# Every fourth column per block: how a graph's turned tile goes through memory and back

## The chip, the core and the metric

The kernel runs on one core of one Trainium2 chip. The metric is the device time of one execution in microseconds (us). The core's engines run their own instruction streams and meet at semaphores: TensorE (PE in the profile), VectorE (DVE), ScalarE (ACT), GpSimd (POOL) and SyncE (SP), which here issues all the DMAs.

## What is computed

Two layers of masked attention with a layer norm ahead of each, on 128 graphs of 128 nodes with 384 features, in float32. Attention has 6 heads of 64.

```python
h = jnp.maximum(_layernorm(x, axis=-1), 0.0)
x = x + _L0_gnn_ref(h, Wq, bq, Wk, bk, Wv, bv, Wf, bf, adj)
h = jnp.maximum(_layernorm(x, axis=-1), 0.0)
x = x + _L1_gnn_ref(h, ...)          # the same with the second set of weights
# in each layer:
scores = jnp.einsum('bhqd,bhkd->bhqk', q, k) / np.sqrt(HEAD_SIZE)
probs = jax.nn.softmax(scores + bias, axis=-1)   # bias: 0 where adj, else -9e15
ctx = jnp.einsum('bhqk,bhkd->bhqd', probs, v)
return ctx @ Wf + bf
```

## The kernel before

A unit `t` is one group of four graphs (`PER`) in one layer; there are 64 units, 256 pairs of a graph and a layer. The two layers of different groups are interleaved. `over_slots` runs `slot(t)` for units 1 to 61 on every engine; each slot has four steps `i`, and each step does work of several graphs at different stages, chosen by `graph_at(t, i, steps)`. The order within a step is written out by hand in the `slot` function of each engine, and for the head and for the last two units (`last_units`) line by line.

Products of float32 data are made as three float16 products of high and low halves. For this each tile is split: ScalarE writes the high half, VectorE or GpSimd the low one.

Two tiles of each graph have to be transposed, with rows on the other axis: `h` (128 nodes x 384 features, the input of the projections) and the probabilities (128 queries x 6 heads x 128 keys, the right side of the context product). VectorE transposes only within blocks of 32 x 32, so the transposition has two parts:

- `turn_blocks` (lines 1229 to 1231; called by `h_turn` and `probs_turn`) turns 32 x 32 blocks on VectorE, from `h` into `h_blocks` or from the probabilities into `p_blocks`. Of each run of 128 columns, block `b` is made of the 32 neighbouring columns 32 b to 32 b + 31.
- the blocks are then moved across partitions by way of memory: `keep_blocks` (lines 356 to 361) writes the tile to `h_dram` or `p_dram` in one DMA, and `bring_back` (363 to 368) reads it into `h_moved` or `p_moved` with four DMAs, one for each group of 32 partitions. `keep_h`, `bring_h`, `keep_probs` and `bring_probs` call them from SyncE's stream.

The read tile is taken by ScalarE (`h_hi`, line 940, and `p_hi`, line 961), then by GpSimd (`h_lo`, 547, and `p_lo`, 552). In the first two units and the last three, where the probabilities aren't split, TensorE reads `p_moved` itself (`apply_probs`, 736). All buffers of this path (`h_blocks`, `h_moved`, `p_blocks`, `p_moved`) are double, by the parity of `i`. Each DMA adds 16 to its semaphore, so `h_back[i]` and `p_back[i]` grow by 64 for each tile.

On VectorE, `slot` runs the turn of the probabilities (line 1230) beside the residual add (1300), the low half of v (1258), the turn of h, the statistics (1225, 1227), the reciprocal of the softmax sums (1254), the masked scores with their minimum (1289), and the low halves of q and k (1269). The last are awaited by TensorE: the projections of q and k have two PSUM banks (`ps_qk`), and the scores of a unit need all six chunks. TensorE's projections and output products are lines 665 to 667, its context product line 759 and its scores line 779.

Of the kernel before, what the change touches and what calls it, by code (L numbers as in the profile page):

```python
# [21 lines left out]
def build(nc, x, adj, layers, out):  # L22
# [23 lines left out]
    SQ = 32  # L46
    QUADS = P // SQ
# [13 lines left out]
    def unit_no(t):  # L61
        return min(t, LAST)
# [17 lines left out]
    def unit_count(t, each=1, plus=0):  # L80
        return each * unit_no(t) + plus
# [10 lines left out]
    def wait(eng, sem, value):  # L92
        if value > 0:
            eng.wait_ge(sem, value)

    def graph_at(t, i, steps):

        return t + (i + steps) // PER, (i + steps) % PER
# [9 lines left out]
    def halved(t):  # L108

        return HALVED <= t < A - 1  # L110

    def halved_count(t, i):
        return PER * (t - HALVED) + i + 1
# [6 lines left out]
    with ExitStack() as ctx:  # L120
# [6 lines left out]
        def sem(name):  # L127
            return ctx.enter_context(nc.semaphore(name))
# [108 lines left out]
        h_back = [sem(f"h_back{i}") for i in range(PER)]  # L237
# [15 lines left out]
        p_back = [sem(f"p_back{i}") for i in range(PER)]  # L253
# [22 lines left out]
        def ctx_bank(i):  # L276
            return ps_shared[i % 2]
# [8 lines left out]
        def v_of(t, i):  # L286
            return v[:, (PER * t + i) % V_SLOTS, :]

        def v_part(t, i, part):
            return v_of(t, i).bitcast(F16)[:, part * H:(part + 1) * H]  # L290

        def p_part(i, part):
            return p_half[i % 2][:, part, :]
# [5 lines left out]
        def first_bank(i):  # L299

            return (ps_qk[0], ps_qk[1], ps_scores[0], ps_scores[1])[i]
# [6 lines left out]
        def moved_in_order(tile):  # L308

            return tile[:, :, :].rearrange("p a (c k) -> p c a k", c=KT)  # L310

        def in_order(view):
            return view.rearrange("p c (a k) -> p c a k", a=QUADS)
# [7 lines left out]
        def _(sp):  # L321
# [33 lines left out]

            def keep_blocks(t, i, blocked, blocks, dram, kept, back):

                wait(sp, back[i], unit_count(t, 16 * QUADS))
                wait(sp, blocked, unit_count(t, PER, i + 1))
                sp.dma_start(dram[i, :, :, :, :].rearrange("a r b n -> (a r) b n"), blocks[i % 2][:, :, :]  # L360
                             ).then_inc(kept[i], 16)

            def bring_back(t, i, dram, moved, kept, back):

                wait(sp, kept[i], unit_count(t, 16, 16))
                for quad in range(QUADS):
                    sp.dma_start(moved[i % 2][quad * SQ:(quad + 1) * SQ, :, :],  # L367
                                 dram[i, :, :, quad, :].rearrange("a r n -> r a n")).then_inc(back[i], 16)

            def keep_probs(t, i):  # L370
                keep_blocks(t, i, p_blocked, p_blocks, p_dram, p_kept, p_back)

            def bring_probs(t, i):
                du, di = graph_at(t, i, -2)
                if halved(du):

                    sp.wait_ge(p_set, halved_count(du, di))
                else:
                    wait(sp, ctx_summed, unit_count(t, PER, i - 1))
                bring_back(t, i, p_dram, p_moved, p_kept, p_back)  # L380

            def keep_h(t, i):

                keep_blocks(t - 1, i, h_blocked, h_blocks, h_dram, h_kept, h_back)
# [241 lines left out]
        def _(pe):  # L626
# [109 lines left out]
            def apply_probs(t, i):  # L736
                vu, vi = graph_at(t, i, 8)
                if i % 2 and vu < B:

                    pe.wait_ge(v_set, unit_count(vu, PER, vi + 1))  # L740
                else:

                    wait(pe, out_added, unit_count(t, PER, i - 1))
                    pe.wait_ge(v_set, unit_count(t, PER, i + 1))
                if (t, i) == (0, 0):
                    pe.wait_ge(largest_taken, LAYERS)
                    pe.wait_ge(out_bias_set, LAYERS)
                if halved(t):
                    pe.wait_ge(p_set, halved_count(t, i))
                    terms = [(v_part(t, i, a), p_part(i, b)) for a, b in ((0, 0), (1, 0), (0, 1))]  # L750
                else:
                    pe.wait_ge(p_back[i], unit_count(t, 16 * QUADS, 16 * QUADS))
                    terms = [(v_of(t, i), p_moved[i % 2][:, :, :].rearrange("p a n -> p (a n)"))]
                for c in range(PAIRS):
                    for k, (values, turned) in enumerate(terms):
                        turned = turned.rearrange("p (a s k) -> p s a k", a=QUADS, s=HEADS)
                        for odd in range(2):
                            hd = 2 * c + odd
                            mm = pe.matmul(ctx_bank(i)[odd * DH:(odd + 1) * DH, c * P:(c + 1) * P],  # L759
                                           values[:, hd * DH:(hd + 1) * DH], turned[:, odd * PAIRS + c, :, :],  # L760
                                           start=k == 0, stop=k == len(terms) - 1)
                mm.then_inc(ctx_summed, 1)
# [148 lines left out]
        def _(act):  # L911
# [17 lines left out]
            def h_hi(t, i):  # L929
                b, rows = unit_no(t) % 2, slice(i * NODES, (i + 1) * NODES)  # L930
                if i == 0:

                    wait(act, qk_projected, unit_count(t - 2, CHUNKS, CHUNKS))
                if t == 0:
                    act.wait_ge(first_turned, i + 1)
                    nc.scalar.activation(ht_hi[0][:, :, rows], first_bank(i)[:, 0:H].rearrange("p (c k) -> p c k", c=KT),
                                         ACT.Copy).then_inc(ht_hi_set, 1)
                    return
                act.wait_ge(h_back[i], unit_count(t - 1, 16 * QUADS, 16 * QUADS))
                nc.scalar.activation(in_order(ht_hi[b][:, :, rows]), moved_in_order(h_moved[i % 2]), ACT.Copy  # L940
                                     ).then_inc(ht_hi_set, 1)

# [12 lines left out]
            def p_hi(t, i):  # L955
                if (t, i) == (HALVED, 0):

                    act.wait_ge(weights_set, CAST_ORDER.index(1) + 1)
                act.wait_ge(p_back[i], unit_count(t, 16 * QUADS, 16 * QUADS))
                act.wait_ge(ctx_summed, unit_count(t, PER, i - 1))  # L960
                nc.scalar.activation(p_part(i, 0), p_moved[i % 2][:, :, :].rearrange("p a n -> p (a n)"), ACT.Copy  # L961
                                     ).then_inc(p_hi_set, 1)
# [158 lines left out]
        def _(dve):  # L1121
# [105 lines left out]
                nc.vector.bn_aggr(mean_var[i % 2][:, :], stats[i % 2][:, :]).then_inc(mean_found, 1)  # L1227

            def turn_blocks(out, view, cols):
                return nc.vector.transpose(out.rearrange("p b (c k) -> p b c k", c=cols),  # L1230
                                           view.rearrange("p (c b r) -> p b c r", c=cols, b=QUADS))

            def h_turn(t, i):
                du, di = graph_at(t, i, -2)
# [269 lines left out]
```

## Time and profile before

| | before |
|---|---|
| median of three runs | 1856.35 us (1855.97 to 1858.41) |
| the profiled execution | 1854.17 us |
| its span, first to last instruction | 1852.4 us |
| mean granted TensorE clock | 0.995 of full speed |
| TensorE, VectorE busy in the span | 98%, 88% |
| ScalarE, GpSimd busy in the span | 84%, 80% |
| DMA engines, mean busy share of the queue SyncE feeds | 65.3% |

The busy time of an engine is that of its instructions in one profiled execution. Matmuls are pipelined, so a busy TensorE has work in flight but isn't at its peak for that. Line numbers are those of the kernel before. "SPq" is SyncE's queue of DMA issues: its times are those of issuing, not of the transfer. The profiled execution stands 2.18 us below the median.

### The profile page before, as it was taken

The numbers are of one execution on the slowest core, as the hardware profiler recorded it, in microseconds if no ns is written. First come the engines' busy times: TensorE is split into PE (matmuls) and PEld (weight loads), VectorE is DVE, ScalarE is ACT, GpSimd is POOL, SyncE is SP. The second block draws the span as 40 slices with busy tenths as digits, with TensorE's granted clock in tenths as the row PEclk, the third lists the DMA queues.
The fourth block names the chain that finished last, engine by engine and source line by source line (L and its number), as shares of the span: only waits on it lengthen the run. The fifth ranks groups of instructions, "written<-read, shape, count | busy, mean of one in ns | idle before, by whom it ended". The sixth has DMA issues, their size and how long they took to land.

```text
span 1852.4 us, 54319 instructions
## 1 busy us (share of the span) xinstructions
PE 1822.2 (98%) x17210; PEld 1050.3 (57%) x17210; DVE 1630.8 (88%) x5555; ACT 1556.1 (84%) x4789; POOL 1485.9 (80%) x1777
## 2 busy tenths in 40 slices
PE   7899999999999999999999999999999999999998
PEld 3455555555555555555555555555555555555555
DVE  7988888899898898988989889888898988889876
ACT  5768888888888888888888888888888888888884
POOL 4668888888888888888888888888888888888772
PEclk8999999999999999999999999999999999999999
DMA  6646766667666666666666666666666666666655
GB/s 193 171 144 198 211 193 196 195 200 212 198 206 189 197 209 203 205 196 194 202 208 204 198 196 201 194 209 205 191 198 197 209 204 200 201 185 189 186 178 182
DMA packets 439943, 363.32 MB, mean 196 GB/s; under 512 B 207701, under 2 KB 406889, under 8 KB 439657
## 3 DMA queue, kind: packets, MB, share of 16 engines
q1 hardware_dynamic: 439656, 359.86, 65.3%
q8 instruction: 137, 2.24, 0.5%
q14 instruction: 150, 1.22, 0.2%
HBM read 184.30 MB, written 175.37 MB: 194 GB/s over the span
## 4 chain that ended last, share of the span: by engine, by line
PE 86%; DVE 4%; DMA 4%; SPq 3%; issue 2%; POOL 1%; ACT 1%; DVEq 0%; POOLq 0%; ACTq 0%
PE ps_qk L665 12%; PE ps_shared L665 12%; PE ps_shared L667 12%; PE ps_shared L666 12%; PE ps_qk L667 12%; PE ps_qk L666 12%; PE ps_shared L759 7%; PE ps_scores L779 7%; SPq L367 3%; DMA p_dram<-p_blocks 2%; DVE probs L1289 1%; DVE p_blocks L1230 1%; DVE qk_lo L1269 1%; POOL probs L540 1%; DMA p_half<-in_L_gnn_Wk 0%
## 5 line engine op out<-in xcount | busy, mean ns | idle before, releaser
L986 ACT ACTIVATE probs<-probs,row_min 128x128 f32<-128x128 f32 x1512 | 583.0, 390 | 2.5 <-DVE row_rcp L1254 1.5
L540 POOL TENSOR_TENSOR probs<-probs,row_rcp 128x768 f32<-128x768 f32 x252 | 371.4, 1474 | 214.1 <-DVE row_rcp L1254 213.9
L1289 DVE CUSTOM_DVE_ANT_0 probs<-ps_scores,mask,minus_scale 128x128 f32<-128x128 f32 x1512 | 429.5, 347 | 0.9 <-issue 0.6
L552 POOL TENSOR_TENSOR p_half<-p_moved,p_half 128x768 f16<-128x768 f32 x236 | 388.0, 1644 | 3.2 <-ACT p_half L961 3.2
L1269 DVE SCALAR_TENSOR_TENSOR qk_lo<-ps_qk,qk_bias,qk_hi 128x512 f16<-128x512 f32 x384 | 277.7, 747 | 60.1 <-ACT qk_hi L969 59.2
L986 ACT ACTIVATION_READ_ACCUMULATOR probs<-probs,row_min 128x1 f32 x1512 | 288.0, 191 | 0.0
L969 ACT ACTIVATE qk_hi<-ps_qk,qk_bias 128x512 f16<-128x512 f32 x384 | 258.3, 673 | 15.1 <-PE ps_qk L667 15.1
L1300 DVE SCALAR_TENSOR_TENSOR x_tile<-ps_shared,out_scale,x_tile 128x384 f32<-128x384 f32 x256 | 157.6, 616 | 123.5 <-PE ps_shared L667 122.1
L536 POOL TENSOR_TENSOR x_tile<-x_tile,out_bias 128x384 f32<-128x384 f32 x256 | 257.8, 1008 | 1.1 <-DVE out_bias L1213 1.1
L665 PE MATMUL ps_shared<-wf_hi,ct_hi 128*128 128x384 f16 x768 | 250.7, 326 | 2.4 <-DVE ct_lo L1263 2.4
L666 PE MATMUL ps_shared<-wf_lo,ct_hi 128*128 128x384 f16 x768 | 250.7, 326 | 0.0
L667 PE MATMUL ps_shared<-wf_hi,ct_lo 128*128 128x384 f16 x768 | 250.6, 326 | 0.0
L665 PE MATMUL ps_shared<-wv_hi,ht_hi 128*128 128x384 f16 x756 | 247.6, 327 | 0.0
L666 PE MATMUL ps_shared<-wv_lo,ht_hi 128*128 128x384 f16 x756 | 247.4, 327 | 0.0
L667 PE MATMUL ps_shared<-wv_hi,ht_lo 128*128 128x384 f16 x756 | 247.4, 327 | 0.0
L1230 DVE STREAM_TRANSPOSE p_blocks<-probs 128x768 f32<-128x768 f32 x252 | 244.0, 968 | 3.7 <-POOL probs L540 3.7
L547 POOL TENSOR_TENSOR ht_lo<-h_moved,ht_hi 128x384 f16<-128x384 f32 x252 | 234.1, 929 | 8.0 <-ACT ht_hi L940 8.0
L948 ACT ACTIVATE v<-ps_shared 128x384 f16<-128x384 f32 x236 | 115.7, 490 | 143.5 <-PE ps_shared L667 142.7
L665 PE MATMUL ps_qk<-ht_hi,wq_hi 128*128 128x512 f16 x576 | 219.7, 381 | 2.1 <-DVE qk_lo L1269 1.8
L665 PE MATMUL ps_qk<-ht_hi,wk_hi 128*128 128x512 f16 x576 | 219.3, 381 | 0.0
L666 PE MATMUL ps_qk<-ht_lo,wq_hi 128*128 128x512 f16 x576 | 218.8, 380 | 0.0
L667 PE MATMUL ps_qk<-ht_hi,wq_lo 128*128 128x512 f16 x576 | 218.8, 380 | 0.0
(144 smaller groups left out, 3973.2 us busy)
## 6 DMA issues: line engine op xcount, KB each, us to landing
p_dram<-p_blocks SPq DMA_DIRECT2D x256, 384.0 KB, 2.4
p_moved<-p_dram SPq DMA_DIRECT2D x1024, 96.0 KB, 2.3
h_dram<-h_blocks SPq DMA_DIRECT2D x252, 192.0 KB, 2.6
h_moved<-h_dram SPq DMA_DIRECT2D x1008, 48.0 KB, 2.0
x_tile<-in_x SPq DMA_DIRECT2D x128, 192.0 KB, 2.9
out_x<-x_tile SPq DMA_DIRECT2D x128, 192.0 KB, 2.7
adj_u<-in_adj SPq DMA_DIRECT2D x64, 64.0 KB, 2.5
wv_raw<-in_L_gnn_Wv SPq DMA_DIRECT2D x2, 576.0 KB, 5.0
```

The source lines that it names most:

```text
L536: nc.gpsimd.tensor_tensor(xs, xs, out_bias[l][:, :], ALU.add).then_inc(res_ready, 1)
L540: nc.gpsimd.tensor_tensor(probs_of(t, i), probs_of(t, i), row_rcp[i % 2][:, :].rearrange("p (a o) -> p a o", o=1) .to_broadcast([P, HEADS, ...
L547: nc.gpsimd.tensor_tensor(in_order(ht_lo[b][:, :, rows]), moved_in_order(h_moved[i % 2]), in_order(ht_hi[b][:, :, rows]), ALU.subtract).th ...
L552: nc.gpsimd.tensor_tensor(p_part(i, 1), p_moved[i % 2][:, :, :].rearrange("p a n -> p (a n)"), p_part(i, 0), ALU.subtract).then_inc(p_set, 1)
L665: pe.matmul(acc, a_hi, b_hi, start=first, stop=False)
L666: pe.matmul(acc, a_hi, b_lo, start=False, stop=False)
L667: return pe.matmul(acc, a_lo, b_hi, start=False, stop=last)
L969: nc.scalar.activation(qk_hi[b][:, chunk, :], ps_qk[chunk % QK_BANKS][:, :], ACT.Identity, bias=qk_bias[layer_of(t)][:, chunk // KT, chunk ...
L986: ins = nc.scalar.activation(tile[:, s, :], tile[:, s, :], ACT.Exp, bias=row_min[i % 2][:, s:s + 1], scale=-1.0, accum_out=row_sum[i % 2][ ...
L1230: return nc.vector.transpose(out.rearrange("p b (c k) -> p b c k", c=cols), view.rearrange("p (c b r) -> p b c r", c=cols, b=QUADS))
L1269: nc.vector.scalar_tensor_tensor(out=qk_lo[b][:, chunk, :], in0=ps_qk[chunk % QK_BANKS][:, :], scalar=qk_bias[layer_of(t)][:, chunk // KT, ...
L1289: ins = nc.vector.tensor_tensor_reduce(tile[:, s, :], score_bank(i, s // PAIRS)[:, (s % PAIRS) * P:(s % PAIRS + 1) * P], mask[b][:, i, :], ...
```

## The change

Block `b` of a run of 128 columns is now made of every fourth column, 4 r + b for r from 0 to 31. VectorE's turn has the same shape and the same output; its input is read with a step of four floats. In memory the row (r, b) of a turned tile then belongs to partition 4 r + b, so the whole tile is one pattern with 128 partitions outermost, and `bring_back` reads it with one DMA. `h_back` and `p_back` grow by 16 for each tile instead of 64, and the waits on them are counted anew. The content of `h_moved` and `p_moved` is the same as before.

```diff
--- before.py
+++ after.py
@@ -355,7 +355,7 @@
 
             def keep_blocks(t, i, blocked, blocks, dram, kept, back):
 
-                wait(sp, back[i], unit_count(t, 16 * QUADS))
+                wait(sp, back[i], unit_count(t, 16))
                 wait(sp, blocked, unit_count(t, PER, i + 1))
                 sp.dma_start(dram[i, :, :, :, :].rearrange("a r b n -> (a r) b n"), blocks[i % 2][:, :, :]
                              ).then_inc(kept[i], 16)
@@ -363,9 +363,8 @@
             def bring_back(t, i, dram, moved, kept, back):
 
                 wait(sp, kept[i], unit_count(t, 16, 16))
-                for quad in range(QUADS):
-                    sp.dma_start(moved[i % 2][quad * SQ:(quad + 1) * SQ, :, :],
-                                 dram[i, :, :, quad, :].rearrange("a r n -> r a n")).then_inc(back[i], 16)
+                sp.dma_start(moved[i % 2][:, :, :], dram[i, :, :, :, :].rearrange("a r b n -> (r b) a n")
+                             ).then_inc(back[i], 16)
 
             def keep_probs(t, i):
                 keep_blocks(t, i, p_blocked, p_blocks, p_dram, p_kept, p_back)
@@ -749,7 +748,7 @@
                     pe.wait_ge(p_set, halved_count(t, i))
                     terms = [(v_part(t, i, a), p_part(i, b)) for a, b in ((0, 0), (1, 0), (0, 1))]
                 else:
-                    pe.wait_ge(p_back[i], unit_count(t, 16 * QUADS, 16 * QUADS))
+                    pe.wait_ge(p_back[i], unit_count(t, 16, 16))
                     terms = [(v_of(t, i), p_moved[i % 2][:, :, :].rearrange("p a n -> p (a n)"))]
                 for c in range(PAIRS):
                     for k, (values, turned) in enumerate(terms):
@@ -936,7 +935,7 @@
                     nc.scalar.activation(ht_hi[0][:, :, rows], first_bank(i)[:, 0:H].rearrange("p (c k) -> p c k", c=KT),
                                          ACT.Copy).then_inc(ht_hi_set, 1)
                     return
-                act.wait_ge(h_back[i], unit_count(t - 1, 16 * QUADS, 16 * QUADS))
+                act.wait_ge(h_back[i], unit_count(t - 1, 16, 16))
                 nc.scalar.activation(in_order(ht_hi[b][:, :, rows]), moved_in_order(h_moved[i % 2]), ACT.Copy
                                      ).then_inc(ht_hi_set, 1)
 
@@ -956,7 +955,7 @@
                 if (t, i) == (HALVED, 0):
 
                     act.wait_ge(weights_set, CAST_ORDER.index(1) + 1)
-                act.wait_ge(p_back[i], unit_count(t, 16 * QUADS, 16 * QUADS))
+                act.wait_ge(p_back[i], unit_count(t, 16, 16))
                 act.wait_ge(ctx_summed, unit_count(t, PER, i - 1))
                 nc.scalar.activation(p_part(i, 0), p_moved[i % 2][:, :, :].rearrange("p a n -> p (a n)"), ACT.Copy
                                      ).then_inc(p_hi_set, 1)
@@ -1227,8 +1226,9 @@
                 nc.vector.bn_aggr(mean_var[i % 2][:, :], stats[i % 2][:, :]).then_inc(mean_found, 1)
 
             def turn_blocks(out, view, cols):
+
                 return nc.vector.transpose(out.rearrange("p b (c k) -> p b c k", c=cols),
-                                           view.rearrange("p (c b r) -> p b c r", c=cols, b=QUADS))
+                                           view.rearrange("p (c r b) -> p b c r", c=cols, b=QUADS))
 
             def h_turn(t, i):
                 du, di = graph_at(t, i, -2)
```

## Rows read from the trace of the kernel before

**Rows 1.** The page, part 1: busy us (share of the span) xinstructions.

```profile
PE 1822.2 (98%) x17210; PEld 1050.3 (57%) x17210; DVE 1630.8 (88%) x5555; ACT 1556.1 (84%) x4789; POOL 1485.9 (80%) x1777
```

**Rows 2.** Windows: stretch, its length, busy us of each engine (xinstructions), clock, DMA share, GB/s.

```profile
0.00:129.50 129.50, 110.96 (x756) 59.13 (x757) 111.56 (x338) 84.28 (x231) 73.04 (x117) 0.93 0.59 174
129.50:185.60 56.10, 53.66 (x522) 31.25 (x521) 47.44 (x163) 46.60 (x145) 45.70 (x55) 1.00 0.63 183
185.60:1756.10 1570.50, 1569.28 (x15115) 908.62 (x15113) 1401.71 (x4811) 1363.35 (x4195) 1322.03 (x1565) 1.00 0.67 199
...
1812.20:1852.40 40.20, 32.20 (x312) 19.75 (x306) 24.37 (x80) 17.02 (x64) 7.14 (x5) 1.00 0.61 197
```

**Rows 3.** Chain that ended last, in order of time: start us, us, what; TensorE's context products.

```profile
178.65 1.13 PE ps_shared L759 x36
...
515.15 1.13 PE ps_shared L759 x36
```

**Rows 4.** VectorE's waits from 185.6 to 1756.1: waited for, us, times, longest.

```profile
DVE x_tile L1300 <- PE ps_shared L667: 112.7, 200, 1.2
DVE qk_lo L1269 <- ACT qk_hi L969: 45.2, 72, 1.6
```

**Rows 5.** TensorE's waits in the same stretch, all of them.

```profile
PE ps_scores L779 <- DVE qk_lo L1269: 1.2, 2, 1.0
```

**Rows 6.** Timeline of SyncE's queue, one graph: start us, us, what, count of issues.

```profile
916.16 0.38 SPq L360 DMA_DIRECT2D p_dram<-p_blocks  x1
...
918.64 1.75 SPq L367 DMA_DIRECT2D p_moved<-p_dram  x4
920.49 1.81 SPq L367 DMA_DIRECT2D h_moved<-h_dram  x4
```

**Rows 7.** The page, part 6: DMA issues, count, KB each, median us from issue to landing.

```profile
p_dram<-p_blocks SPq DMA_DIRECT2D x256, 384.0 KB, 2.4
p_moved<-p_dram SPq DMA_DIRECT2D x1024, 96.0 KB, 2.3
...
h_moved<-h_dram SPq DMA_DIRECT2D x1008, 48.0 KB, 2.0
...
wv_raw<-in_L_gnn_Wv SPq DMA_DIRECT2D x2, 576.0 KB, 5.0
```

**Rows 8.** ScalarE's waits for the reads, from 185.6 to 1756.1.

```profile
ACT p_half L961 <- DMA p_moved<-p_dram: 10.2, 24, 1.1
ACT ht_hi L940 <- DMA h_moved<-h_dram: 9.0, 20, 0.9
```

**Rows 9.** Chain that ended last, the tail: start us, us, what.

```profile
1836.32 2.67 DMA p_dram<-p_blocks
...
1843.07 2.21 DMA p_moved<-p_dram
...
1845.41 0.88 PE ps_shared L759 x12
```

**Rows 10.** Timeline of the tail: start us, us, what, [idle before, releaser].

```profile
1836.47 0.98 DVE L1230 STREAM_TRANSPOSE p_blocks<-x_tile 128x768 f32<-128x768 f32 x1 [0.80 <-POOL x_tile L540]
...
1842.81 0.33 PE L667 MATMUL ps_shared<-wf_hi,ct_lo 128*128 128x384 f16 x1
```

**Rows 11.** ScalarE's waits from 129 to 186.

```profile
ACT p_half L961 <- DMA p_moved<-p_dram: 6.0, 4, 3.8
```

**Rows 12.** Groups by form: line, engine, operation, xcount | busy us, mean ns | idle before.

```profile
L1230 DVE STREAM_TRANSPOSE p_blocks<-probs 128x768 f32<-128x768 f32 x252 | 244.0, 968 | 3.7 <-POOL probs L540 3.7
...
L1230 DVE STREAM_TRANSPOSE h_blocks<-h 128x384 f32<-128x384 f32 x252 | 139.2, 552 | 2.2 <-ACT h L926 2.2
...
L1207 DVE SCALAR_TENSOR_TENSOR wv_lo<-wv_raw,w_scale,wv_hi 128x1152 f16<-128x1152 f32 x2 | 3.9, 1933 | 0.0
...
L1207 DVE SCALAR_TENSOR_TENSOR wk_lo<-wk_raw,w_scale,wk_hi 128x1152 f16<-128x1152 f32 x1 | 2.4, 2437 | 0.0
...
L1207 DVE SCALAR_TENSOR_TENSOR wk_lo<-p_half,w_scale,wk_hi 128x1152 f16<-128x1152 f32 x1 | 1.4, 1386 | 0.0
```

## The prediction, made before the changed kernel was run

> **What bounds the kernel now.** The page comes first: TensorE (PE) is busy for 1822.2 of 1852.4 us, VectorE (DVE) for 1630.8 [rows 1]. A share of the span mixes stages, so the windows come next. From 185.6 to 1756.1 us TensorE has work in flight for 1569.28 of 1570.5 us at full granted clock, VectorE for 1401.71, ScalarE for 1363.35, GpSimd for 1322.03 [rows 2]. TensorE's context product of a pair of graphs recurs every (515.15 - 178.65) / 24 = 14.02 us [rows 3], so one graph of one layer takes 7.011 us and the stretch holds 224 of them. VectorE works 1401.71 / 224 = 6.258 us of each and idles 0.753. The waits say what that idle time is: 112.7 us on TensorE's output product, 45.2 us on ScalarE's high half of q and k [rows 4]. TensorE itself waited 1.2 us in all, for VectorE [rows 5]. So in the steady stretch TensorE sets the pace, no transfer does, and VectorE is second with 11% to spare. Only outside is anything to be gained: TensorE's idle time is 129.5 - 110.96 = 18.5 us in the head, 2.4 us from 129.5 to 185.6, and 40.2 - 32.2 = 8.0 us in the tail [rows 2].
>
> **Edit 1: one read instead of four.** SyncE issues the four reads of a probabilities tile in 1.75 us and the four of an h tile in 1.81 us [rows 6]; there are 1024 and 1008 of them [rows 7]. Each is a quarter of the partitions, with as many runs of 768 or 384 bytes in all as the one read will have. One issue of a whole tile costs about 0.38 us [rows 6] (its row is the write of a tile). So SyncE gives back 1.75 + 1.81 - 2 x 0.38 = 2.8 us of its 7.0 per graph. In the steady stretch that is worth nothing on the path: TensorE doesn't wait for a transfer, and ScalarE waits 10.2 and 9.0 us in 224 graphs [rows 5, 8]; SyncE just waits longer for what comes next. When does the tile land? Now the last of four is issued about 1.3 us after the first and lands 2.3 us later, 3.6 us in all. The same 384 KB as one write land in 2.4 us; 576 KB of weights took 5.0 us in the crowded head [rows 7]. I take 2.4 to 3.6, by the write, its nearest row: the tile is back 0 to 1.2 us sooner. Should it take 5, ScalarE waits 1.4 us longer for a copy, and the head and tail lose what I credit below.
>
> In the tail the issues are on the path. The chain runs from a write issued at 1836.32 to a read issued at 1843.07 [rows 9]; after the write has landed, at 1839.0, SyncE issues eight reads in turn, 8 x 0.5 us, the last at 1843.07. With one read each, the last tile's write follows its block turn (started 1836.47, so done at 1837.45 [rows 10]), lands about 2.67 us on at 1840.2, its read lands 2.2 to 2.9 us later, at 1842.4 to 1843.1, instead of 1845.28. What is late next is TensorE: its last output product of the graphs before starts at 1842.81 [rows 10], then comes a context product of 0.88 us, so the last one starts at 1843.8 rather than 1845.41 [rows 9]: 1.6 us won. At 129.5 to 185.6 one copy waited 3.8 us for a read and TensorE lost 2.4 us, of which 0 to 2.4 come back [rows 2, 11]. The stray 1.2 us of the steady stretch adds 0 to 1.2. The head is a chain of VectorE and weight loads, where I credit nothing. Sum: 1.6 to 5.2 us won, about 4. The smaller semaphore counts cost nothing.
>
> **Edit 2: the turn reads every fourth column.** The count of turns stays: 256 of 768 elements and 252 of 384. Their reads change from runs of 32 neighbouring floats to floats 16 bytes apart. Their writes don't change. Today they take 968 and 552 ns, so (968 - 552) / 384 = 1.083 ns per element beside a fixed part of about 136 ns [rows 12]. No row of the trace shows VectorE reading at such a step, so I bound it. Below, nothing is added: the element count is the same, and a gain is excluded, since the run of neighbours already moves one element per slope. Above, the slowest VectorE row per element is the split of Wk, 2437 ns for 1152 elements or 2.12 ns, where the same operation elsewhere took 1386 [rows 12]; a rate of 2.12 to 2.17, twice the present slope, is my upper row bound. I take the upper end: the nearest thing to a read that touches a fresh place for each element is a read that gets half its rate, and the rows of contiguous reads at the other end are rows of another pattern. Added: 768 x 1.083 = 0.832 us and 384 x 1.083 = 0.416 us, 1.248 us per graph.
>
> VectorE's slack is 0.753 us per graph, so edit 2 costs nothing as long as it adds under 0.753 / 1152 = 0.65 ns per element; 1.083 is past that. VectorE's sum becomes 6.258 + 1.248 = 7.506 us against TensorE's 7.011, and VectorE sets the pace. Behind each longer turn are queued the statistics, the reciprocal, the masked scores and the low halves of q and k, and TensorE's projections wait for those low halves, because their PSUM banks are only two. SyncE's write of a tile waits for the turn as well, but edit 1 has freed more than that.
>
> The Trainium skill bears on this. "SBUF — State Buffer" (section Door 1, the DMA port swizzle) says that accesses in one 16-byte line run at full rate and each that crosses to a new line pays; it gives no price, and it speaks against this change, which has one float per line. "Vector Engine (DVE) Microarchitecture Reference" (section 5.2) gives 1.7 to 2.5 ns per column for a source without adjacent pairs, against 1.05. The trace has no such read; the sum by it would be 0.8 to 1.7 us per graph.
>
> **The whole, for the forecast.** VectorE's work 1630.8 + 256 x 0.832 + 252 x 0.416 = 1948.6 us. Its idle time in head and tail stays, since other things cause it: (129.5 - 111.56) + (40.2 - 24.37) = 33.8 us. That makes 1982. Of the steady idle time, the 112.7 us on TensorE vanish with TensorE's lead; of the 45.2 us on ScalarE between none and all stays, say half: 23. Then 2005, less 3 for edit 1: span 2002. The profiled execution took 1854.17 for a span of 1852.4, and the median of three is 1856.35, 2.2 above it; so 2002 + 1.8 + 2.2 = 2006 us. Own range: 1980 to 2040, the top for waits between engines that now have little slack.
>
> **Rivals.**
> - *The turn stays as fast (the other side).* Then only edit 1 is left: 1854.2 + 2.2 - 4 = 1852 us, 1848 to 1856. It holds from 0 up to about 0.4 ns per element. For it: the turn streams one element at a time anyway, and its slope is VectorE's ordinary one. Against: nothing in the trace shows a spaced read. Chance 0.25.
> - *A part price, near the tipping point.* Splitting Wv ran at 1933 / 1152 = 1.68 ns per element [rows 12], 0.6 above the turn's slope. VectorE's sum is then 6.258 + 0.69 = 6.95 us, just under TensorE's 7.011, but the 45.2 / 224 = 0.20 us of waits for ScalarE don't go away: 7.15, or +0.14 x 224 = 31 us; with up to 0.8 us added per graph it is 7.26, +56 us. So 1875 to 1935, about 1905. Its page is the microarchitecture reference of the Trainium skill named above, with the lower of its prices. Chance 0.27.
> - *More than double.* At 1.5 ns more per element VectorE's sum is 6.258 + 1.73 = 7.99 us, with 0.1 of handoffs 8.1, +244 us and some 15 in head and tail: 2080 to 2140. No row supports it; the higher price of the same page does. Chance 0.13.
> - *The single read lands later than four did* (over 5 us): at most a few us, in head and tail, within each case.
>
> **How the numbers follow.** Forecast 0.35, rivals 0.25, 0.27 and 0.13. The forecast is the likeliest, 2006. The range 1848 to 2045 takes in the fast case, the part price and the forecast and leaves out the last rival and the edges. A measurement of this kernel can tell 0.2%, 3.7 us. The fast case straddles that bound: faster 0.14, within it 0.10. Slower: 0.76.
>
> **What would show it.** In the profile after: the two turn groups at about 1800 and 968 ns (right), or unchanged at 968 and 552 (first rival), or about 1430 and 780 (second). VectorE's share over 95% with TensorE's near 91%, and VectorE's waits on the output product gone; TensorE waiting for the low halves of q and k. Reads: 256 and 252, one issue near 0.4 us, landing in 2.4 to 3.6 us. The last read would be issued near 2.7 us after the last write. The prediction is wrong if the turns keep their time, or if VectorE is slower and TensorE still isn't made to wait.

## The result, and the profile after

The changed kernel takes 1887.45 us (median of four runs, 1884.65 to 1890.59) against 1856.16 us: a ratio of 1.0168, 95% interval 1.0155 to 1.018. It is 31 us slower. The profiled execution took 1890.59 us for a span of 1888.8 us. The prediction said slower, and 2006 us. The time is that of its second rival, the part price near the tipping point (1875 to 1935 us).

The page of the changed kernel, part 1 (as rows 1), then VectorE's turns by form (as rows 12):

```profile
PE 1845.0 (98%) x17210; PEld 1044.5 (55%) x17210; DVE 1831.8 (97%) x5555; ACT 1551.9 (82%) x4789; POOL 1485.9 (79%) x1777
```

```profile
L1230 DVE STREAM_TRANSPOSE p_blocks<-probs 128x768 f32<-128x768 f32 x252 | 396.5, 1573 | 3.4 <-POOL probs L539 3.4
...
L1230 DVE STREAM_TRANSPOSE h_blocks<-h 128x384 f32<-128x384 f32 x252 | 220.0, 873 | 1.2 <-ACT h L925 1.2
```

TensorE's busy share is 98% as before, which is where a reader goes wrong first: busy only says that some matmul is in flight, and the count of matmuls below shows what the share hides. VectorE has gone from 88% to 97%. The turns take 1573 and 873 ns instead of 968 and 552 [rows 12]: 605 ns more for 768 elements and 321 for 384, 0.79 and 0.84 ns per element.

Windows of the changed kernel (columns as in rows 2):

```profile
0.00:129.50 129.50, 107.03 (x724) 56.43 (x725) 115.40 (x318) 80.98 (x216) 68.69 (x111) 0.92 0.55 168
129.50:185.60 56.10, 54.26 (x523) 31.14 (x521) 53.57 (x165) 45.13 (x145) 43.69 (x55) 1.00 0.58 178
185.60:1756.10 1570.50, 1565.37 (x14885) 888.92 (x14884) 1558.82 (x4752) 1341.26 (x4141) 1307.70 (x1546) 1.00 0.63 197
```

All that VectorE waited for from 185.6 to 1756.1 us, in the list of waits (as rows 4), and then what TensorE waited for in it (as rows 5):

```profile
DVE qk_lo L1269 <- ACT qk_hi L968: 2.3, 6, 0.6
DVE probs L1289 <- issue: 0.6, 2, 0.3
DVE row_rcp L1254 <- issue: 0.5, 2, 0.3
DVE ct_lo L1263 <- issue: 0.2, 1, 0.2
```

```profile
PE ps_shared L664 <- DVE ct_lo L1263: 3.5, 10, 0.6
PE ps_scores L778 <- DVE qk_lo L1269: 1.2, 4, 0.4
```

In the steady stretch VectorE is busy for 1558.82 of 1570.5 us, 99.3%. Its 112.7 us of waits for TensorE's output product [rows 4] are gone altogether, and those for ScalarE have shrunk from 45.2 to 2.3. The chain of work that ended last has moved from TensorE to VectorE. Its shares of the span by engine (part 4 of the page), before and after:

```profile
PE 86%; DVE 4%; DMA 4%; SPq 3%; issue 2%; POOL 1%; ACT 1%; DVEq 0%; POOLq 0%; ACTq 0%
```

```profile
DVE 61%; PE 24%; issue 8%; DMA 3%; POOL 2%; ACT 1%; DVEq 0%; POOLq 0%; SPq 0%; ACTq 0%
```

TensorE's named waits are still only 4.7 us, so the loss has to be read from the count of matmuls: TensorE started 14885 in the stretch. The unhindered pace is 15122 or 15123 in 1570.5 us (the same window of four kernels below), that is 67.5 for each of 224 graphs. By that measure 14885 are 220.5 graphs, 7.12 us each instead of 7.01. (By VectorE's own count, 4752 instructions at 21.5 per graph, it is 221.0 graphs and 7.11 us: a count at the edges of a window can be off by part of a graph.)

The same counts place the loss. Up to 1756.1 us the kernel before had started 756 + 522 + 15115 = 16393 matmuls [rows 2] and the changed one 724 + 523 + 14885 = 16132. The 261 missing are 27.1 us at 9.63 per us: 3.2 us were lost before 185.6 us (1247 matmuls against 1278) and 23.9 in the steady stretch. The span of the profiled execution grew by 36.4 us, so 9.3 us were lost in the tail. Some 3 of these are TensorE's clock, by an estimate from the spacing of the matmuls: after idling for 2.35 us it was granted 0.50 of its clock from 1860 to 1863 us and ran its products 0.32 us apart instead of 0.16, and again near 0.57 from 1880 to 1884, after 1.35 and 1.52 us of idling. (By the medians the loss is 31.3 us, so these parts belong to one execution, somewhat longer than most.)

The changed kernel's DMA issues, part 6 of its page (as rows 7), and then the end of its chain (as rows 9):

```profile
p_dram<-p_blocks SPq DMA_DIRECT2D x256, 384.0 KB, 2.4
p_moved<-p_dram SPq DMA_DIRECT2D x256, 384.0 KB, 3.7
h_dram<-h_blocks SPq DMA_DIRECT2D x252, 192.0 KB, 2.1
h_moved<-h_dram SPq DMA_DIRECT2D x252, 192.0 KB, 3.7
```

```profile
1871.45 3.82 DMA p_dram<-p_blocks
1875.33 4.72 DMA p_moved<-p_dram
```

The single reads land 3.7 us after their issue, for 384 KB as for 192 KB, where the last of four landed 1.3 + 2.3 = 3.6 us after the first was issued. So the tile isn't back any sooner. SyncE is freed as foreseen, and waits for the turns instead: 881 us in the steady stretch, where it was 69.

### The profile page after: what moved, and what is told of

Read it like the earlier page. It is cut to its first block, busy times and chain, and to the rows that moved or that the text cites. A ratio compares the mean times of both kernels' runs of the same rounds, so it can differ in the third digit from the quotient of the medians.

```text
span 1888.8 us, 52795 instructions
## 1 busy us (share of the span) xinstructions
PE 1845.0 (98%) x17210; PEld 1044.5 (55%) x17210; DVE 1831.8 (97%) x5555; ACT 1551.9 (82%) x4789; POOL 1485.9 (79%) x1777
## 4 chain that ended last, share of the span: by engine, by line
DVE 61%; PE 24%; issue 8%; DMA 3%; POOL 2%; ACT 1%; DVEq 0%; POOLq 0%; SPq 0%; ACTq 0%
DVE probs L1289 14%; DVE p_blocks L1230 13%; DVE qk_lo L1269 9%; DVE h_blocks L1230 7%; DVE ct_lo L1263 4%; DVE stats L1224 4%; PE ps_shared L664 4%; DVE x_tile L1300 3%; PE ps_shared L666 3%; PE ps_shared L665 3%; PE ps_qk L664 3%; PE ps_qk L665 3%; PE ps_qk L666 3%; DVE v L1258 3%; PE ps_shared L758 2%
## 5 line engine op out<-in xcount | busy, mean ns | idle before, releaser
L1230 DVE STREAM_TRANSPOSE p_blocks<-probs 128x768 f32<-128x768 f32 x252 | 396.5, 1573 | 3.4 <-POOL probs L539 3.4
L1230 DVE STREAM_TRANSPOSE h_blocks<-h 128x384 f32<-128x384 f32 x252 | 220.0, 873 | 1.2 <-ACT h L925 1.2
```

## The experiments

Two theories. **A:** the whole loss is VectorE's time; it shows only where VectorE's sum per graph passes TensorE's. **B:** part of it comes with the single read (a later landing) or with the spaced access as such (a port or bank that others share, a place in the order).

### Each half alone

One read with the turn of before:

```diff
-                                           view.rearrange("p (c r b) -> p b c r", c=cols, b=QUADS))
+                                           view.rearrange("p (c b r) -> p b c r", c=cols, b=QUADS))
```

> The changed kernel with the turn of before (runs of 32 neighbouring columns): only the one read instead of four is left. The partitions of the turned tiles then hold features and keys in another order, so the result isn't the reference's; all work is done. Theory A (the loss is VectorE's time): turns back at 968 and 552 ns, VectorE's steady idle time of about 0.75 us per graph is back, and the time is that of the kernel before within 0.3%: 1850 to 1861 us. Theory B (the single read, which lands 3.7 us after its issue, does harm of its own in head, tail or both): slower than before by 5 to 30 us, 1861 to 1886.

Measured: 1851.84 us, ratio 0.9977 (0.9968 to 0.9987). Edit 1 alone is worth 4 us.

The spaced turn with the four reads of before (the same line, the other way round, in the kernel before):

> The kernel before with the turn of the change (every fourth column) and its four reads: only the dearer turn is left. Features and keys stand in another order, so the result isn't the reference's. Theory A: turns at 1573 and 873 ns, VectorE busy for 97% and slower by 20 to 31 us, 1876 to 1887 us. Theory B: less than half of the loss is here, 1856 to 1870.

Measured: 1889.93 us, ratio 1.0182 (1.0167 to 1.0197). The turns are at 1573 and 872 ns. The whole loss is in edit 2; theory B's first form falls. (The time is 3 us above the range that was expected.) With the dear turn in place, edit 1 is worth 1889.93 - 1887.45 = 2.5 us, no more than the two medians can tell.

Windows of the kernel with one read and the turn of before, and then the end of its chain (start, length, what ran):

```profile
0.00:129.50 129.50, 110.22 (x759) 59.11 (x760) 111.86 (x342) 85.27 (x232) 74.10 (x117) 0.95 0.58 178
129.50:185.60 56.10, 56.10 (x535) 32.57 (x534) 49.91 (x171) 48.64 (x152) 47.22 (x57) 1.00 0.60 187
185.60:1756.10 1570.50, 1570.50 (x15123) 909.93 (x15122) 1401.64 (x4816) 1358.59 (x4200) 1325.06 (x1568) 1.00 0.64 200
```

```profile
1832.82 4.28 DMA p_dram<-p_blocks
...
1837.16 4.75 DMA p_moved<-p_dram
...
1843.12 0.43 PE ps_shared L664
1843.55 0.32 PE ps_shared L665
```

The gain is at the start of the steady stretch: from 129.5 to 185.6 TensorE is busy for all 56.1 us instead of 53.66 [rows 2], and at 1756.1 it is 24 matmuls, 2.5 us, ahead. The tail gives nothing more, for two reasons. The last turn starts at 1831.77 instead of 1836.47 [rows 10], but the last write lands 4.28 us after its issue and the last read 4.75, against 2.67 and 2.21 [rows 9], so the last context product starts at 1842.05 instead of 1845.41: 3.4 us sooner, of which 2.5 were won ahead of the tail. And TensorE, which had idled for 1.39 and 1.35 us before its last two context products, runs the first nine of the eighteen matmuls that follow 0.32 us apart instead of 0.16: from 1844 to 1846 us the granted clock was 0.50, the level of 1.2 GHz, where it was 1.00 before (idle times there: 0.48 and 0.91 us). That costs about 1.6 us.

### Each tile alone: is there a threshold?

`bring_back` and `turn_blocks` choose by tile; the waits count 16 or 64 accordingly:

```diff
+        H_READS, P_READS = 1, 4          # the other kernel: 4, 1
...
+                reads = H_READS if cols == KT else P_READS
+                order = "p (c r b) -> p b c r" if reads == 1 else "p (c b r) -> p b c r"
```

> The change for the h tiles alone (spaced turn, one read); the probabilities as before. VectorE gets 0.32 us more per graph, under its idle time of 0.75. Theory A with the threshold: steady stretch unchanged, 1853 to 1860 us. If every ns on VectorE costs in proportion, a third of the 31 us: 1864 to 1868.

> The change for the probabilities alone; the h tiles as before. VectorE gets 0.61 us more per graph, still under 0.75. Theory A with the threshold: the steady stretch hardly moves, 0 to 4 us there, and head and tail lose some, 1857 to 1868 us. In proportion, two thirds of 31 us: 1875 to 1879.

Measured: h alone 1856.86 us, ratio 1.0009 (1.0 to 1.0019); the probabilities alone 1861.84 us, 1.0027 (1.0014 to 1.004). The two together cost 31 us, singly 1 to 2 us (h alone, hardly clear of noise) and 5 to 6 us. The costs don't add, as a threshold asks and a price in proportion forbids. Windows of the two kernels, h alone and then the probabilities alone:

```profile
185.60:1756.10 1570.50, 1570.50 (x15123) 909.84 (x15121) 1470.04 (x4812) 1358.37 (x4200) 1322.87 (x1568) 1.00 0.65 200
```

```profile
185.60:1756.10 1570.50, 1570.50 (x15122) 909.64 (x15121) 1521.48 (x4811) 1360.64 (x4198) 1323.78 (x1565) 1.00 0.65 200
```

TensorE starts 15123 and 15122 matmuls: the steady stretch lost nothing, though VectorE works 68 and 120 us more in it than in the kernel before.

### The same time without a spaced access, and the spaced access without the time

The kernel before, turning each probabilities tile twice, contiguous:

```diff
+                turn_blocks(p_blocks[i % 2][:, :, :], probs_of(t, i).rearrange("p a k -> p (a k)"), HEADS).then_inc(turned_once, 1)
+                wait(dve, turned_once, unit_count(t, PER, i + 1))
                 turn_blocks(p_blocks[i % 2][:, :, :], probs_of(t, i).rearrange("p a k -> p (a k)"), HEADS
                             ).then_inc(p_blocked, 1)
```

> The kernel before, but VectorE turns each probabilities tile twice in a row, contiguous both times (four reads, results as before). It adds 0.97 us and a short wait to VectorE per graph, with no spaced access anywhere. If it is VectorE's time alone that counts (theory A), this acts like the change and a little more, since 1.0 is above 0.93: slower by 2 to 4%, 1890 to 1925 us. If the spaced reads hurt by another way (a port or bank that other engines share), it costs clearly less than the change, under 1.5%.

Measured: 1911.92 us, ratio 1.0302 (1.0284 to 1.0319). A contiguous 0.974 us plus its wait costs more than the spaced 0.926. No port or bank is needed to explain the change.

The changed kernel with VectorE relieved elsewhere:

```diff
-                nc.vector.scalar_tensor_tensor(out=xs, in0=out_bank(i)[:, 0:H], scalar=out_scale[l][:, :], in1=xs,
+                nc.vector.scalar_tensor_tensor(out=xs[:, 0:32], in0=out_bank(i)[:, 0:32], scalar=out_scale[l][:, :], in1=xs[:, 0:32],
```

> The changed kernel, but VectorE adds the residual only for 32 of 384 columns of each graph; the other columns of the output keep the input, so the result isn't the reference's. VectorE does about 0.35 us less per graph and everything else stays, the spaced turns too. Theory A (TensorE against VectorE, whichever has more per graph): VectorE falls from 7.07 to about 6.7 us, below TensorE's 7.01; the steady loss goes, and 5 to 14 us of head and tail stay: 1858 to 1870 us. If the spaced turn hurts by its place in the order (a later write, a later read) rather than by VectorE's sum, it stays near 1887.

Measured: 1861.38 us, ratio 1.003 (1.0019 to 1.0042). The spaced turns are all there, and 26 of the 31 us are gone. The window of the steady stretch of this kernel, then of the one that turns twice, then the last two windows of the kernel with the spaced turn and four reads (its first window has 719 matmuls):

```profile
185.60:1756.10 1570.50, 1570.50 (x15122) 909.74 (x15121) 1517.51 (x4815) 1359.82 (x4201) 1324.37 (x1564) 1.00 0.64 200
```

```profile
185.60:1756.10 1570.50, 1551.57 (x14762) 879.07 (x14757) 1553.28 (x4908) 1330.88 (x4094) 1291.39 (x1531) 1.00 0.65 195
```

```profile
129.50:185.60 56.10, 52.69 (x452) 29.27 (x451) 52.24 (x166) 43.89 (x136) 42.40 (x50) 1.00 0.60 178
185.60:1756.10 1570.50, 1566.52 (x14948) 889.84 (x14947) 1560.06 (x4753) 1346.53 (x4143) 1310.07 (x1548) 1.00 0.65 197
```

Read together (graphs in the stretch = matmuls / 67.5; VectorE's work = its busy time / graphs; pace = 1570.5 / graphs):

| kernel | VectorE per graph, us | pace, us | ratio of the time |
|---|---|---|---|
| before | 6.26 | 7.01 | 1 |
| h alone | 6.56 | 7.01 | 1.0009 |
| residual cut, change kept | 6.77 | 7.01 | 1.003 |
| probabilities alone | 6.79 | 7.01 | 1.0027 |
| spaced turn, four reads | 7.04 | 7.09 | 1.0182 |
| the change | 7.07 | 7.12 | 1.0168 |
| turned twice | 7.10 | 7.18 | 1.0302 |

Theory A holds over the whole table: TensorE's 7.01 us stand until VectorE's sum reaches them, and then the pace is VectorE's sum and about 1%. (The two kernels with both spaced turns have in truth one pace, 7.11 us: VectorE runs 4753 and 4752 instructions in the stretch. The 7.09 and 7.12 come from where the edges of the stretch cut TensorE's work: at 185.6 us TensorE had started 1171 and 1247 matmuls, at 1756.1 16119 and 16132.) For each tile alone the small loss is in the tail, where turns are on the chain: up to 1756.1 us these two kernels had started 16390 and 16404 matmuls, the kernel before 16393. For the residual cut 2.2 of the 6.6 us between the profiled executions come before the tail (16372), the rest in it.

### What a step costs: a price list

Single operations with a wait after each, behind the end of the kernel before. For instance, for a step of two:

```diff
+            for _ in range(REPEAT):
+                then(nc.vector.transpose(dst[:, 0:768].rearrange("p (b c k) -> p b c k", c=12, b=2), src[:, 0:768].rearrange("p (c r b) -> p b c r", c=12, b=2)))
```

> The kernel before with a list of single operations behind its end, each six times (four on GpSimd) with a wait between them: VectorE's turn of 768 and 384 elements with neighbours, and with steps of 4, 2, 3, 8 and 24 floats, the turn with a spaced output, a scaling and a sum with and without a step of 4; on ScalarE a copy with spaced input or output, on GpSimd a sum. If what counts is two neighbouring words (one rule of the skill), a step of 2 floats costs as much as 4: about 1570 ns. If what counts is two hits in a line of 16 bytes (the other), a step of 2 is free, 968 ns, a step of 3 lies between, and 4, 8 and 24 cost the same, about 1570. The total time says nothing; it is some 60 us above the kernel before.

The groups by form behind the kernel's end; they are listed by busy time and told apart by their line: the turn of 768 with neighbours (L1520), of 384 with neighbours (L1522), of 768 with a step of 4 (L1524), of 384 with a step of 4 (L1526), then of 768 with steps of 2 (L1528), 3 (L1530), 8 (L1532) and 24 (L1534), with a spaced output (L1536); a sum with neighbours and with one input at a step of 4 (L1542, L1544). Then ScalarE's copy: plain, spaced input, spaced output (L1139, L1143, L1147); GpSimd's sum: plain, spaced output (L632, L636).

```profile
L1534 DVE STREAM_TRANSPOSE wq_raw<-wf_raw 128x768 f32<-128x768 f32 x6 | 12.5, 2085 | 0.2
L1143 ACT ACTIVATE wk_raw<-wf_raw 128x768 f32<-128x768 f32 x6 | 9.4, 1569 | 0.2
L1532 DVE STREAM_TRANSPOSE wq_raw<-wf_raw 128x768 f32<-128x768 f32 x6 | 9.3, 1549 | 0.2
L1147 ACT ACTIVATE wk_raw<-wf_raw 128x768 f32<-128x768 f32 x6 | 9.3, 1548 | 0.2
L1524 DVE STREAM_TRANSPOSE wq_raw<-wf_raw 128x768 f32<-128x768 f32 x6 | 9.2, 1532 | 0.2
L1536 DVE STREAM_TRANSPOSE wq_raw<-wf_raw 128x768 f32<-128x768 f32 x6 | 9.2, 1528 | 0.2
L1544 DVE TENSOR_TENSOR wq_raw<-wf_raw 128x768 f32<-128x768 f32 x6 | 9.1, 1516 | 0.2
L1530 DVE STREAM_TRANSPOSE wq_raw<-wf_raw 128x768 f32<-128x768 f32 x6 | 7.2, 1193 | 0.2
L636 POOL TENSOR_TENSOR wv_raw<-wf_raw 128x768 f32<-128x768 f32 x4 | 6.3, 1564 | 0.3
L1528 DVE STREAM_TRANSPOSE wq_raw<-wf_raw 128x768 f32<-128x768 f32 x6 | 5.9, 979 | 0.2
L632 POOL TENSOR_TENSOR wv_raw<-wf_raw 128x768 f32<-128x768 f32 x4 | 5.9, 1466 | 107.7 <-DVE wq_raw L1545 107.5
L1520 DVE STREAM_TRANSPOSE wq_raw<-wf_raw 128x768 f32<-128x768 f32 x6 | 5.9, 976 | 0.2
L1542 DVE TENSOR_TENSOR wq_raw<-wf_raw 128x768 f32<-128x768 f32 x6 | 5.8, 958 | 0.2
L1526 DVE STREAM_TRANSPOSE wq_raw<-wf_raw 128x384 f32<-128x384 f32 x6 | 5.1, 854 | 0.2
...
L1139 ACT ACTIVATE wk_raw<-wf_raw 128x768 f32<-128x768 f32 x6 | 5.1, 842 | 97.1 <-DVE wq_raw L1545 96.9
L1522 DVE STREAM_TRANSPOSE wq_raw<-wf_raw 128x384 f32<-128x384 f32 x6 | 3.5, 579 | 0.2
```

A step of two floats is free (979 ns against 976), a step of three costs 217 ns, a step of four 556, eight 573, and 24 costs 1109. VectorE's scaling of 768 elements, in the list but not among the rows shown, goes from 560 to 845 ns with an input at a step of 4. Up to the step of eight that fits a price for each fresh 16 bytes once every element needs its own, as "SBUF — State Buffer" of the Trainium skill (section Door 1, the DMA port swizzle) has it, and not for lost neighbours (the further rise at 24 is not explained by it): "Vector Engine (DVE) Microarchitecture Reference" of the Trainium skill, section 5.2, would have a step of two pay as well, and the measurement decides against that here. Its 1.7 ns per column for a source that hops does agree with the step of four: (1532 - 854) / 384 = 1.77 ns, against (976 - 579) / 384 = 1.03.

### Can the order be had for nothing? Four tries

**The order provided for elsewhere.** The turn of before and one read; rows of Wq, Wk and Wv loaded in the order of the features, and the scores taking the keys with a step of four:

```diff
-                                           k[b][rows, KT + c, cols], start=first, stop=last)
+                                           k[b][rows, KT + c, cols].rearrange("p (r b) -> p b r", b=QUADS), start=first, stop=last)
...
+                    sp.dma_start(w_raw[l][j][:, c, :],
+                                 layers[l]["W" + NAMES[j]][c * P:(c + 1) * P, :].rearrange("(b r) n -> r b n", b=QUADS)
+                                 ).then_inc(w_loaded[l][j], 16)
```

> The one read of the change with the turn of before. The order that the read gives is provided for elsewhere: each group of 128 rows of Wq, Wk and Wv is loaded in the order in which the features come back (three loads of 192 KB instead of one of 576 KB), h of unit 0 is written by ScalarE in that order, and the scores take the keys with a step of four (TensorE's moving operand, 8 bytes apart), as does the mask on ScalarE, so that the keys come back in order. Theory A: VectorE's work is that of before, so 0.2 to 0.4% faster than before, 1848 to 1853 us. If TensorE pays for the spaced keys, the score products get longer than 219 ns and the time rises with them, since TensorE sets the pace: each 10 ns on 4608 of them is up to 20 us.

Measured: 1983.63 us, ratio 1.0693 (1.0677 to 1.0709). Score products in the timeline of the kernel before, around 907 us, and of this one:

```profile
907.01 0.22 PE L779 MATMUL ps_scores<-qk_lo,qk_hi 64*128 64x128 f16 x2
907.07 0.22 PE L779 MATMUL ps_scores<-qk_hi,qk_lo 64*128 64x128 f16 x2
```

```profile
907.35 0.29 PE L784 MATMUL ps_scores<-qk_lo,qk_hi 64*128 64x128 f16 x2
907.47 0.30 PE L784 MATMUL ps_scores<-qk_hi,qk_lo 64*128 64x128 f16 x2
```

A pair of them (one of each half of the array) starts every 0.12 us instead of every 0.06. With 2304 pairs that is some 140 us, and 128 were measured. TensorE sets the pace, so all of it counts. (No run has the spaced keys alone; the other edits of this kernel are in it too.) The step here is 8 bytes, which VectorE's turn gets for nothing.

**A step of two, two reads.** A block takes every second column of 64; a half tile comes back with each read:

```diff
+                return nc.vector.transpose(out.rearrange("p (x y) (c k) -> p c x y k", c=cols, x=2),
+                                           view.rearrange("p (c x r y) -> p c x y r", c=cols, x=2, y=2))
...
+                for half in range(2):
+                    sp.dma_start(moved[i % 2][half * 2 * SQ:(half + 1) * 2 * SQ, :, :],
+                                 dram[i, half, :, :, :, :].rearrange("a r y n -> (r y) a n")).then_inc(back[i], 16)
```

> The change with a step of two floats instead of four, for both tiles: a block takes every second column of 64, so that half a tile comes back with one read, two reads in all (the write to memory goes out in twice as many runs of half the length). By the price list a turn with a step of 2 costs 979 ns against 976: turns at about 970 and 552 to 580 ns, and VectorE keeps its idle time. Half of what the single read gave: 0.1 to 0.3% faster than before, 1850 to 1855 us. If the price list doesn't hold under load (turns over 1100 ns), slower than before.

Measured: 1855.38 us, ratio 0.9999 (0.999 to 1.0007). Its turns, then its reads and writes:

```profile
L1246 DVE STREAM_TRANSPOSE p_blocks<-probs 128x768 f32<-128x768 f32 x252 | 243.9, 968 | 3.7 <-POOL probs L553 3.7
...
L1246 DVE STREAM_TRANSPOSE h_blocks<-h 128x384 f32<-128x384 f32 x252 | 139.0, 551 | 2.2 <-ACT h L939 2.2
```

```profile
p_dram<-p_blocks SPq DMA_DIRECT2D x256, 384.0 KB, 2.9
p_moved<-p_dram SPq DMA_DIRECT2D x512, 192.0 KB, 3.5
```

The turns cost nothing more, under load too. But the half of the gain that I expected isn't there: each half tile lands 3.5 us after its issue, the second later than the last of four did.

**h alone, by the order of the weights' rows, with and without the step of two for the probabilities:**

> The probabilities as in e8_step_two (step of two, two reads); h with the turn of before and one read, its order of features provided for by the order in which the rows of Wq, Wk and Wv are loaded, and by ScalarE's write of h in unit 0. Turns at 970 and 552 ns; SyncE issues three reads per graph instead of eight. Between e8_step_two and e1_one_read: 0.15 to 0.3% faster than before, 1849 to 1854 us.

> Only the h part of e9_step_two_h_order: one read for h with neighbours turned and the rows of the weights in that order; the probabilities with four reads as before. If the gain of e1_one_read is in the tail, where only probabilities are left, it isn't here: within 0.1% of before, 1854 to 1858 us. If it is SyncE's freed time anywhere, 0.1 to 0.2% faster.

Measured: 1856.28 us, ratio 1.0007 (0.9998 to 1.0015), and 1855.34 us, 0.9998 (0.9989 to 1.0007). Neither gains. **The probabilities alone with one read**, the turn of before:

> The turn of before for both tiles; the probabilities with one read, h with four. The keys come back in another order, so the result isn't the reference's. It tells where the gain of e1_one_read (0.23%) comes from, since one read for h alone gave nothing: if from the probabilities, 0.15 to 0.3% faster than before, 1850 to 1853 us; if only from both together (SyncE's whole freed time), within 0.1%, 1854 to 1857 us.

Measured: 1853.96 us, ratio 0.9992 (0.9983 to 1.0001). So a gain is clear of noise only with both tiles on one read (0.23%); one read for h gave nothing, and one for the probabilities 0.08% (-0.01 to 0.17%), so whether that read alone gives part of the gain isn't shown. Which of SyncE's waits it frees at 130 to 180 us was not isolated. Of the versions that keep the features in the order that the products want, none is measurably faster than the kernel before; the free step of two gives the same time with half the reads.

## Why the prediction was right or wrong

- **What bounds the kernel:** right. TensorE's 7.01 us per graph and VectorE's distance to it decided everything, and VectorE's waits on TensorE vanished as foretold. Those on ScalarE, of which half was to stay, went too.
- **The direction, and its mechanism:** right; VectorE's sum passed TensorE's (7.07 us against 7.01).
- **The step that failed is the price of the spaced turn.** I doubled the slope, by the slowest VectorE row per element: +1.083 ns. Measured: +0.79 and +0.84 ns, 0.926 us per graph and not 1.248. The split of Wk had nothing to do with a step, and durations of such splits aren't the price of an access at all: in the changed kernel, where they are the same instructions, those of Wv took 1484 ns instead of 1933 and one of Wq 2130 instead of 1599. Over the kernel that is 1630.8 + 256 x 0.605 + 252 x 0.321 = 1866.6 us of VectorE work and not 1948.6: 82 us too much.
- **VectorE's sum was also too high by 35 us:** it came out at 1831.8 and not 1866.6. VectorE's instructions overlap when they follow without a wait, by some 0.09 us, and busy time counts an overlap once. The durations of its 5555 instructions, added up over all groups, rose from 2022 to 2259 us, 237 us, nearly all of it the turns' 236; the busy time rose by only 201, so 36 us more are overlap. The forecast added the turns' time as if none of it could overlap. The probable reason is that idle gaps have gone: the 278 of the steady stretch have become 11, and 267 x 0.09 = 24 us. That reason is read from the profile, not isolated by a run, and h alone doesn't fit it well: it lost 104 gaps, and the overlap gave back 0.01 us per graph where the count would give 0.04. In the timeline of the changed kernel:

```profile
916.46 1.58 DVE L1230 STREAM_TRANSPOSE p_blocks<-probs 128x768 f32<-128x768 f32 x1
917.95 0.59 DVE L1300 SCALAR_TENSOR_TENSOR x_tile<-ps_shared,out_scale,x_tile 128x384 f32<-128x384 f32 x1
```

  The turn that starts at 916.46 ends at 918.04, and the next instruction starts at 917.95.
- **The threshold** (0.753 us of slack) was therefore too low. By durations added up, the change should have brought VectorE to 6.26 + 0.93 = 7.19 us per graph; it came to 7.07. The 0.12 us that the overlap gave back belong to the slack, which makes it near 0.87. That is an estimate: the turned-twice kernel and the change with 0.93 and more lie past the threshold, the probabilities alone with 0.61 below, and no run lies between.
- **The idle time that stays** was right in sum, by luck: 33.8 + 23 = 57 us, measured 1888.8 - 1831.8 = 57.0. Its parts were not. In the steady stretch 11.7 us stayed and not 23. Outside it 45.3 us stayed and not 33.8: the sum had left out the stretches from 129.5 to 185.6 us and from 1756.1 to 1812.2, where VectorE had idled for 8.7 and 10.4 us before. The two misses of VectorE's work explain the difference: 82 + 35 = 117 us, less the 3 that were credited for edit 1, against 2002 - 1888.8 = 113.
- **The signs:** the chain shows TensorE made to wait, but not by the signs that the prediction named. TensorE's share stayed at 98%, not near 91%, and its named waits are 4.7 us, most of them for the low half of the context and not of q and k. Read by busy share and waits alone, the last line of the prediction would have called its own mechanism wrong. The turns were to take 1800 and 968 ns and took 1573 and 873; the last read was issued 3.9 us after the last write, not 2.7.
- **Edit 1 alone:** the size was right (4 us forecast, 3.9 measured), its places half. The 2.4 us from 129.5 to 185.6 came; the 1.6 us of the tail didn't. The forecast held the last turn where it was, and that started 4.7 us sooner; but the write after it took 4.28 us, not 2.67, and the single read 4.75, not the 2.2 to 2.9 that I took from a write. What was left of the gain, 0.9 us, went with the lower clock of the last products. The row of a write isn't that of a read in four times as many runs.
- **The choice of the case:** the part price was the case with a row beside it (1.68 ns, the split of Wv) and with the page's lower price. I gave it 0.27 and took the doubled slope with 0.35. The measured price, 0.79 to 0.84 ns more, lies between the two (0.6 and 1.083). That the part price named 31 us and 31 came is partly luck: its VectorE sum stayed below TensorE's, 6.95 us, and it reached 7.15 by waits for ScalarE that are gone in the trace, while the measured sum is above, 7.07. The range held because it reached across both.

## What to carry to other kernels

Before giving a second engine more work, put its sum per iteration beside that of the engine that sets the pace: up to the difference the work is nearly free, and past it each further 0.01 us counts in full. VectorE's turn of float32 may step over one element for nothing (979 ns against 976), but not over two or three (1193, 1532). When an engine's busy share looks unchanged, count its instructions in a fixed window of the steady stretch instead.

## What the runs showed of the hardware that was not expected

- VectorE's turn with a step of two floats costs 979 ns against 976, with four 1532, with 24 2085; a spaced output costs as much as a spaced input (1528).
- The price is not VectorE's alone: ScalarE's copy of 768 goes from 842 to 1569 ns with a step of four, GpSimd's sum with a spaced output only from 1466 to 1564.
- TensorE pays for float16 columns 8 bytes apart in its moving operand: pairs of 64-row products every 0.12 us instead of 0.06.
- With both tiles on one read, the reads of 384 KB and of 192 KB (512 runs each) both land 3.6 to 3.7 us after their issue, while the same 384 KB written in 128 runs lands in 2.4 to 2.5. That isn't set by the count of runs alone: with the probabilities in four reads, the same single read of h lands in 2.7 to 2.8 us (the h order alone and h alone), and with h in four reads that of the probabilities in 3.9 to 4.0.
- TensorE's granted clock fell to 0.50 in the tail of the kernel with one read and the turn of before, after two idle times of 1.39 and 1.35 us close together; idle times of 0.48 and 0.91 us at the same place in the kernel before left it at 1.00.
